# A three-stage transformer kernel on one core: the order of work at two entries and of one copy in a DMA queue

## The reference, cut to what matters

```python
def moe(x):                                   # E=8 experts, CAP=320 slots each, F=1024
    tokens = layernorm(x).reshape(-1, 256)
    probs  = softmax(tokens @ gate_w)
    expert = argmax(probs)                    # slots are given out in the order of the tokens
    h   = relu(expert_input @ w1[e])          # gathered rows, 256 -> 1024
    out = h @ w2[e]                           # 1024 -> 256, scattered back, times prob
x = x + 0.5 * moe(x)

h = layernorm(x)
k, v, q = (conv4(h @ W.T) for W in (Wk, Wv, Wq))          # causal, 4 taps, width 64
alpha, eta, theta = rates(h)                              # sigmoid, sigmoid, softplus, mean of 64
for chunk in 8 chunks of 128 tokens:                      # per batch
    g = clip(grad of |silu(k W1.T) W2.T - v|^2 at the W that holds when the chunk begins)
    S_t = eta_t S_(t-1) - theta_t g_t ;  W_t = (1 - alpha_t) W_(t-1) + S_t
    y_t = silu(q_t W1_t.T) W2_t.T
x = x + rms(y @ Wo.T) * norm_g * (h @ gW.T + gb)
x = x + 0.5 * moe(x)
```

## Time and profile before

| what | us |
| --- | --- |
| median of 3 runs | 777.61 |
| the runs | 777.61, 771.98, 778.47 |
| the profiled execution | 779.93 |
| its span, first to last instruction | 778.1 |
| busy: TensorE, VectorE, ScalarE, GpSimd | 666.3, 607.7, 436.2, 238.4 |
| mean granted TensorE clock, share of full | 0.947 |

### The profile page before, as it was taken

The page is one execution under the profiler, slowest core; times in us unless marked ns, Lnnn a source line. Parts: engine busy times, 40 slices in busy tenths (PEclk is TensorE's granted clock), DMA queues, the critical chain, the costliest instruction groups (busy, mean ns, idle before and its releaser), DMA issues. The chain is left out here.

```text
span 778.1 us, 15439 instructions
## 1 busy us (share of the span) xinstructions
PE 666.3 (86%) x5697; PEld 578.9 (74%) x5697; DVE 607.7 (78%) x1369; ACT 436.2 (56%) x1102; POOL 238.4 (31%) x201
## 2 busy tenths in 40 slices
PE   4439989999597899999999999999977258999996
PEld 2128879898476787979888798888865047989985
DVE  0867768873489999999999999999866659887851
ACT  1505475562466676677776767776633426457550
POOL 0033713113212234070432506143241054711202
PEclk9859999999799999999999999999969579999998
DMA  9968717260411013031130502203030715724301
GB/s 339 424 208 302 257 63 251 61 187 28 130 40 55 1 47 118 1 109 56 56 109 2 163 1 87 78 2 109 1 104 12 264 44 167 277 79 179 128 14 35
DMA packets 58226, 89.26 MB, mean 115 GB/s; under 512 B 6960, under 2 KB 49072, under 8 KB 58032
## 3 DMA queue, kind: packets, MB, share of 16 engines
q1 hardware_dynamic: 46176, 70.28, 26.0%
q0 software_dynamic: 3840, 10.49, 4.1%
q10 hardware_dynamic: 8144, 7.61, 3.3%
HBM read 74.73 MB, written 22.02 MB: 124 GB/s over the span
## 5 line engine op out<-in xcount | busy, mean ns | idle before, releaser
L662 PE MATMUL ps<-moe_normedT_high,weights_high_up 128*128 128x320 f32 x256 | 82.9, 324 | 7.8 <-DVE moe_normedT_low L470 4.0
L1156 POOL TENSOR_TENSOR att_o_rs<-att_o_mean,minus_half 128x4 f32<-128x4 f32 x16 | 17.2, 1076 | 205.5 <-DVE att_o_mean L1413 205.5
L663 PE MATMUL ps<-moe_normedT_low,weights_high_up 128*128 128x320 f32 x256 | 79.7, 311 | 0.0
L664 PE MATMUL ps<-moe_normedT_high,weights_low_up 128*128 128x320 f32 x256 | 79.7, 311 | 0.0
L500 DVE SCALAR_TENSOR_TENSOR moe_hidden_low<-ps,moe_hidden_high 128x256 fp32r<-128x256 f32 x128 | 53.9, 421 | 29.6 <-ACT moe_hidden_high L622 23.2
L662 PE MATMUL ps<-weights_high_down,moe_hidden_high 128*128 128x256 f32 x256 | 73.3, 286 | 0.0
L664 PE MATMUL ps<-weights_high_down,moe_hidden_low 128*128 128x256 f32 x256 | 71.5, 279 | 0.0
L663 PE MATMUL ps<-weights_low_down,moe_hidden_high 128*128 128x256 f32 x256 | 71.4, 279 | 0.0
L596 ACT CAST weights_high_down<-weights_raw_down 128x256 fp32r<-128x256 f32 x96 | 35.1, 407 | 40.5 <-PE ps L664 26.4
L662 PEld LDWEIGHTS ps<-moe_normedT_high,weights_high_up 128*128 128x128 f32 x256 | 49.0, 191 | 10.4 <-DVE moe_normedT_low L470 4.5
L621 ACT ACTIVATE moe_shared<-ps 128x64 f32<-128x64 f32 x128 | 28.8, 225 | 40.0 <-PE ps L664 35.3
(11 more groups left out here) (301 smaller groups left out, 2050.8 us busy)
## 6 DMA issues: line engine op xcount, KB each, us to landing
weights_raw_up<-in_w SPq DMA_DIRECT2D x16, 1024.0 KB
weights_raw_down<-in_w SPq DMA_DIRECT2D x16, 1024.0 KB
first_xt<-in_xT SPq DMA_DIRECT2D x8, 1024.0 KB, 7.8
weights_rows<-x SPq DMA_DIRECT2D x8, 1024.0 KB, 5.4
out_x<-weights_rows SPq DMA_DIRECT2D x8, 1024.0 KB, 4.4
weights_rows<-x ACTq DMA_DIRECT2D x7, 1024.0 KB, 5.5
weights_rows<-x SPq DMA_DIRECT2D x2, 512.0 KB, 4.2
weights_raw_up<-in_w_x SPq DMA_DIRECT2D x1, 768.0 KB
```

The source lines that it names most:

```text
L662: mm(dst, high_l, high_r, start=start, stop=False)
L663: mm(dst, high_l, low_r, start=False, stop=False)
L664: return mm(dst, low_l, high_r, start=False, stop=stop)
L1156: g.tensor_tensor(o_rs[:, n], o_mean[:, n], t["minus_half"][:, n], ALU.pow).then_inc(o_rs_ready, 1)
```

## The change

Five places change; no arithmetic does.

- `experts`, SP's list: the second half of the copy of x is issued ahead of pair 1's UP loads instead of behind them. (The second pass has no copy.)
- Attention entry, ScalarE: the first four batches are normalised ahead of the copy of the turned state (`first_normalise` ahead of `new_turned`).
- Attention entry, TensorE: x is turned ahead of `gram`.
- Step 0, VectorE: the carry scans go from ahead of the split of x to behind the gradient norms, followed by the decay scans and softplus; the statistics of chunk 2 go from behind the norms to behind the gradients.
- Step 0, GpSimd: query decay and mix of chunk 0 go from ahead of the gradient's power to behind it.

```diff
@@ experts, sync
-            units(1, UP)
             if x_copy is not None:
                 sp.dma_start(*x_copy).then_inc(copied, 16)
+            units(1, UP)
             units(1, DOWN)
@@ memory_attention, gpsimd
             def step(c, par, first, last, norm_too=True):
                 gradient_norm(c)
-                if not first and not last:
+                if first:
+                    query_decay(c, True)
+                    mix(c, True)
+                elif not last:
                     hidden(c, par, False)
...
             hidden(0, 0, True)
-            query_decay(0, True)
-            mix(0, True)
             step(0, 0, True, False)
@@ memory_attention, vector
                 split_turned(c + 1)
-                if first:
-                    decay_scans(c, True)
-                else:
+                if not first:
                     slope_of(c)
...
                 gradient_norms(c, par)
-                if norm_too:
+                if first:
+                    carry_scans(c, True)
+                    decay_scans(c, True)
+                    softplus(c, par)
+                elif norm_too:
                     stats_of(c + 2)
-                if first:
-                    softplus(c, par)
                 thetas(c, par)
                 gradients(c, par)
+                if first:
+                    stats_of(c + 2)
                 convolve_first(c + 1, 1 - par)
...
             key_norms(0, 0, first_k_sq)
-            carry_scans(0, True)
             step(0, 0, True)
@@ memory_attention, scalar
+            first_normalise()
             new_turned(0)
-            first_normalise()
             turned(0, True)
@@ memory_attention, tensor
             unread_products(5, 1, DD)
+            turn_x(0, True)
             gram(0)
-            turn_x(0, True)
             pe.wait_ge(x_turned_split, 1)
```

## The result

| | median, us | runs | ratio of the fast runs, 95% interval |
| --- | --- | --- | --- |
| kernel before, same chip | 777.72 | 20 | |
| changed kernel | 781.84 | 20 | 1.0053 [1.0039, 1.0068] |

The change costs 4.1 us (3.0 to 5.3) where 0.8 us of gain was forecast. The profiled execution of the changed kernel took 777.01 us, the least of its 20, and that of the kernel before 779.93, more than its median. So their totals say nothing, and the profile is read stage by stage. Ratios leave out executions more than 1.5% above the fastest of the same kernel; this weighs most where step 0 alone is changed, as 6 of its 12 fall out, the profiled one among them.

What follows compares the result with a forecast made beforehand. VectorE was taken to bound the attention steps (44.1 of 46.15 us busy), full DMA engines and unstopping TensorE the first experts pass. Entry -1.34, step 0 +0.8, loop's entry -0.3: -0.8 on 777.61 gives 776.8 us, range 772.3 to 780.6.

Steps and rivals of the forecast that it cites:

- Part 1: Attention entry: normalising and first projection come earlier, -1.34 us in full, -0.4 if gram falls on the path.
- Part 2: Step 0 of the attention: four differences on VectorE's chain, +0.8 us, ends +0.1 and +1.5.
- (a): Step 0, VectorE: the split comes first and VectorE idles until ScalarE's copy is done, +0.7 us.
- (b): Step 0, VectorE: gradient norms take 2.5 us instead of 3.69 with GpSimd idle, -1.1 us.
- (c): Step 0, VectorE: theta scale, factor and grad_w1 wait beside GpSimd's products, +1.6 us, ends 0 and +2.2.
- the 0.48 of waiting for the last gates: Late in step 0: a late VectorE no longer waits 0.48 us for TensorE's last gate pair, leaving +0.8.
- the other chain: Step 0, if (c) costs nothing: ScalarE's query tap waits for query decay, delaying rates and last tap 1.5 to 2 us.
- That gain is swallowed: Step 0, TensorE: projections start at 243.9 instead of 245.74, then wait for ScalarE's copy of the keys; no gain.
- Part 3: First experts pass, SP's queue: copy lands about 67.5, loads just fit, gathers come about 70; -0.3 us.
- rival B: First experts pass: copy lands at 72.6, first load too late for ScalarE; +3.0 us, 780.6, chance 0.16.
- The gain of 0.3 us: Expert loop's entry: a tenth of the 2.7 us between the first and second run of the code, -0.3.
- rival A: Expert loop's entry: 2.7 us owed to late gathers and scatters come back, step 0 costs 0.1; 773.7, chance 0.16.

Runs made afterwards that it cites:

- copy alone: Only the copy of x moved ahead of the second pair's up loads, against the kernel before: 0.9999 and 1.0007, pooled 1.0004 [0.9980, 1.0027].
- three repetitions: The changed kernel run again unaltered, against the kernel before: 1.0023, 1.0026 and 1.0046.
- kernel with the 13 matmuls: Changed kernel plus 13 unread matmuls on TensorE between step 0's last projection and its rates; against the kernel before 0.9997 and 1.0013.
- tanh first: Changed kernel with ScalarE's tanh of the rates ahead of its query tap in step 0; against the kernel before 1.0008 and 1.0068, pooled 1.0031.
- entry alone: Kernel before with only the attention entry's part of the change: 0.9962, 0.9976 and 0.996, pooled 0.9963 [0.9947, 0.9979].
- entry and copy: Changed kernel without its part in step 0, which keeps the order before; against the kernel before 0.9982 [0.9947, 1.0016].
- carry scans back: The tanh first kernel with the carry scans put back ahead of the split in step 0; ratio 1.0011 [0.9978, 1.0043].
- copy last: Kernel before with the second half of the copy of x behind all four loads of the second pair; ratio 1.0019 [0.9996, 1.0042].

## Why the prediction was wrong, point by point

**Part 1** had the mechanism right: -1.34 forecast, -1.22 in the profile, and gram lay in the wait as said. That the size fits is in part luck: it was read off a profile with the clock at 0.50 there, and the same unchanged entry took 40.03 and 39.65 us where it was 0.85 and 1.00.

**Part 2** had the order of events right and failed in one step. (a) 0.69 us of idle time, as forecast. (b) The norms took 2.46 us instead of 3.69: -1.2, forecast -1.1. (c) Theta scale 1.50 instead of 0.17, factor 0.47 instead of 0.17, grad_w1 1.07 instead of 0.69: +2.0, forecast +1.6. The forecast counted three instructions with two SBUF inputs; the theta scale, one of the three, has one (att_theta_sum), and grew most all the same. The first taps are 1.66 us late (18.90 us behind the key norms instead of 17.24), forecast 1.2. With the clock held up, the stage is 43.25, +1.27: inside the forecast's ends for this part (+0.1 to +1.5), and the 0.48 of waiting for the last gates was absorbed as it said.

**The failed step** is the sentence on the other chain: ScalarE's query tap "drags sigmoid, rates and last tap by 1.5 to 2 us", and then only an alternative to (c), priced at nothing beside it. The wait was named, and the late start was sized about right: the query tap ended 2.4 us late (14.38 us behind the key norms, 252.41-238.03; before 11.99), forecast 1.9, and the rates started 1.87 late. But they ended 3.67 late, not 1.5 to 2. What was not asked is what TensorE does meanwhile: it starts later and has finished 0.7 us earlier, so its wait grows from both ends, 1.25 to 3.83 us, and behind it the rates run at half clock, 1.8 us more. "That gain is swallowed" was right for 1.0 of the 1.7 us by which the projections start earlier; the other 0.7 was priced at 0 and lengthened the idle time. Nowhere does the forecast ask for the clock: that term stood at nothing, and it was 1.7 us of the stage. In all six profiles with that wait of 3.8 us the rates took 3.17 to 3.79 us; in all others 1.99.

**Part 3** was off in size. The copy landed at 69.3, forecast 67.5: "11.7, plus 1.5 of start" was 15.5, and no run shows the 1.5 by itself. GpSimd's gathers came at 74.22, forecast about 70. The first load needed the 4.7 us that the forecast had as its most, and landed at 74.0, past the 73.4 from which rival B was to decide. Rival B's mechanism is there, a ScalarE that waits for a DMA (0.88 us in the changed kernel's first profile, 2.30 in the copy alone) and a first middle up to 3.5 us late (28.63 us in place of 25.11). That is its price at this place, but not in the time: the copy alone is at +0.3 (-1.6 to +2.1). The gain of 0.3 us stood on a difference within that comes and goes from profile to profile without the copy's doing; rival A rested on the same rows.

**What stays open.** Entry and step 0 together add 1.75 us in the first profile (-1.22+2.97), and 0.83, 0.92 and 2.06 in the three repetitions (39.37+44.07, 39.32+44.21 and 39.29+45.38 against 82.61). The pooled time is +3.6 us (2.7 to 4.5). The kernel with the 13 matmuls is at +0.2 (-1.2 to +1.6), 3.4 us less, where its step 0 gives 0.8 to 2.1. Against this stands the tanh first, of the same stage, at +2.4. The entry alone has a gap of its own: -2.9 us in time (-4.1 to -1.6), of which its stage gives at most 1.4. Wait and clock are shown as the largest part that has a place; some 2 us have none. A part of them can be the copy's (up to 2 us by its own interval), a part the executions that no profile shows: the first expert product starts at 52.8 to 57.1 us, and from step 0 to the second pass's first middle it is 371.5 to 379.7 us, in kernels that don't differ there.

## What to carry to other kernels

When a change makes one engine finish earlier, look at what it waits for next: if that has not moved, or moves the other way, the gain becomes idle time, and on TensorE idle time can be charged twice. In a step where one engine is busy nearly all along (VectorE here, 40.8 of 42.0 us), reordering can win little unless it takes away busy time: count the collisions with GpSimd before and after. A gain read off one profile holds for the clock of that profile: look at the same stage in others. Test the parts of a bundled change by themselves: the entry alone measured 2 to 3 us faster, and the whole 4 slower.

## What the runs showed of the hardware that was not expected

- In step 0 TensorE's granted clock fell to 0.5 at or behind a wait of 3.8 us in six of six profiles, behind a wait of 3.23 us in five of nine, and never behind the waits of 1.25. Of the five, entry and copy and carry scans back had some 12 of 36 projections at 0.63 us instead of 0.39; the entry alone (two of its three profiles) and the copy last had about 8, and their step 0 took 42.22 to 42.24 us instead of 41.98. With the waits filled by unread matmuls the clock stayed at 1.00 in three of three. The Trainium skill, TensorE: Matmul & The Clock Gate, section "Part 1: The HAM clock gate (the "warmup" mystery)", says that the throttled clock is the idle state and that, at a kernel's start, the number of slow matmuls differs between runs of one kernel. That the same 3.23 us wait cost clock in some profiles only agrees with it. A projection of the entry alone behind that wait:

```profile
246.99 0.63 PE L1806 MATMUL ps<-att_xT_low,att_w_high 128*128 128x512 f32 x1
```

The row of the entry-and-copy kernel, whose step 0 is that of the kernel before and took 43.29 us instead of 41.98, and that of a profile of the entry alone in which the clock held, at the same place:

```profile
245.00:250.00 5.00, 3.29 (x8) 2.61 (x9) 5.00 (x5) 4.89 (x7) 0.00 (x0) 0.56 0.59 198
```

```profile
245.00:250.00 5.00, 3.19 (x14) 2.60 (x15) 5.00 (x4) 4.89 (x8) 0.00 (x0) 1.00 0.64 201
```

- An instruction with 8 elements on VectorE took 2.21 us beside GpSimd's product of 2.40 (0.17 alone). The Trainium skill, SBUF — State Buffer, section "Who interferes with whom", has it that a VectorE instruction with two SBUF inputs and a GpSimd one that reads SBUF contend for a shared port pair, under an exclusive lock; the rows here agree, for 8 elements a partition as for the 512 of grad_w1 (1.07 instead of 0.69). The theta scale has one SBUF input and took 1.50 us instead of 0.17 beside such a product.
- A transfer of 4.2 MB ahead of two of 1 MB made their landing 19.7 to 21.6 us instead of 5.0 to 8.4, with gathers beside both.
